# Delta of a masked-softmax graph layer turned by VectorE in 32x32 blocks and dealt through HBM, with the scores placed after the second projection

## The chip, the cores and the metric

The kernel runs on one core of a Trainium2 chip. The metric is the device time of one execution in microseconds. The engines are named as in the profile: PE (TensorE), ACT (ScalarE), DVE (VectorE), POOL (GpSimd) and SP (SyncE, which only issues the DMAs here). The name of an engine with a small q is its sequencer or queue.

## What is computed

32 batches of 256 nodes with 384 features. For each batch, from x (256 x 384) and an adjacency matrix (256 x 256, about 3% ones):

```python
u = h @ h.T / sqrt(384)
p = softmax(u, axis=-1)
delta = p * adjacency
attn = delta / (delta.sum(axis=2, keepdims=True) + 1e-10)
h_left, h_self, h_right = h @ W_left.T + b_left, h @ W_self.T + b_self, h @ W_right.T + b_right
ctx = triu(attn, 1) @ h_left + diag(attn)[:, None] * h_self + tril(attn, -1) @ h_right
o = layernorm(ctx) * gamma + beta          # eps 1e-12
out = layernorm(x + relu(o))               # eps 1e-5
```

Everything is float32. The kernel leaves out the division by the softmax sum and by the row sum of delta: the layer norm that follows is blind to the scale of a row, so only its epsilon is scaled. What PE multiplies is split into a high and a low part (fp32r), and each product is three passes: high by high, high by low, low by high.

## The kernel before

A batch is two row tiles (T = 2) of 128 nodes; features are three chunks (C = 3) of 128. The batches run one after the other in a loop unrolled four times (`every_batch`, UNROLL = 4). Each engine has its own program in a fixed order, in which `at` is the batch at hand, `nxt` the one after it, `before` and `second` the one and the two before; semaphores tie the programs together, and nothing is reordered at run time. So the order of the calls in the five functions `one` is the order of the work.

PE, for each batch (`one`, L329): the left and right projection of row tile 0 (`project` 0 and 1, 9 matmuls of 384 columns each), `turn_delta` (L297: delta is [row, neighbour] and is wanted as [neighbour, row], so four 128x128 blocks are transposed into the PSUM tile ps_dt), projections 2 to 5 (left and right of row tile 1, then self of both), `scores` of the next batch (18 matmuls of 256 columns), and `attend` for both row tiles (9 matmuls of 386 columns each, which accumulate on ps_ctx). A projection starts on a PSUM bank (`ps_proj`, four banks in a ring) that ACT has seeded with the bias (`seed_proj`, L359), and `attend` on a ps_ctx that ACT has seeded with the self projection times the diagonal of delta (`seed_ctx`, L380).

ACT (`one`, L418) writes the high part of each of the first four projections (`split_proj`), of delta transposed (`split_delta`, L376) and of the next batch's x (`split_xt`), seeds the banks, takes the exponentials of the next batch in place (`exps`, L351), normalises the batch before (`normalise`) and writes the output of the second before (`outputs`).

DVE (`one`, L552) writes the low parts, takes the row maxima of the scores (`maxima`), forms delta (`deltas`, L461), sums its diagonal blocks against an identity (`diagonal`), and does the statistics of both layer norms (`context_stats`, `norm_shift`, `residual`, `residual_stats`). POOL (`one`, L634) raises the variances to -1/2 (`power`, tile rstd), multiplies by gamma (scaled), adds beta (shifted), and cuts the two diagonal blocks of delta transposed into strict triangles with two selects (`triangles`, L614; the first matmul of `attend` waits for them).

SP (`one`, L250): once the residual of the second batch before is formed, three loads (x transposed, x, adjacency) into the ring of four; then the store of the second batch's output. Ahead of the loop it issues the first batches' loads and the weights one after the other.

Of the kernel before, what the change touches and what calls it, by code (L numbers as in the profile page):

```python
# [22 lines left out]
P = 128  # L23
UNROLL = 4
# [49 lines left out]
def gnn_resnorm(nc, x, x_t, adj, wt_left, b_left, wt_self, b_self, wt_right, b_right, gamma, beta, out):  # L74
# [14 lines left out]
    BLOCKS = [(0, 0), (1, 1), (1, 0), (0, 1)]  # L89
    FULL, MASK_LEFT, MASK_RIGHT = range(3)  # L90
    ATTEND = [
        [(MASK_LEFT, 0, 0), (MASK_RIGHT, 0, 1), (FULL, 2, 2)],
        [(FULL, 3, 1), (MASK_LEFT, 1, 2), (MASK_RIGHT, 1, 3)],
    ]

    with ExitStack() as ctx:
# [24 lines left out]
        xt_hi = [sb(f"xt_hi{i}", [P, C, L], F32R) for i in range(2)]  # L121
        xt_lo = [sb(f"xt_lo{i}", [P, C, L], F32R) for i in range(2)]
# [8 lines left out]
        on_diag = sb("on_diag", [P, T, P])  # L131

# [14 lines left out]
        rstd = sb("rstd", [P, 2 * T])  # L147
        shift = sb("shift", [P, 2 * T])
# [7 lines left out]
        ps_dt = psum("ps_dt", [P, T * T, P])  # L156
# [22 lines left out]
        dt_ready = sem("dt_ready")  # L179
# [42 lines left out]

        block = ctx.enter_context(nc.Block())

        @block.sync
        def _(sp):
# [16 lines left out]
            for b in range(1, UNROLL):  # L243
                load(b, b)
# [22 lines left out]
        def _(pe):  # L267
# [7 lines left out]
            def xt(at, c, a, b):  # L275
                par = at.slot(2)
# [47 lines left out]
            for _ in range(WARM_UP):  # L324
                nc.tensor.transpose(ps_dt[:, 0, :], ident[:], ident[:])
# [3 lines left out]
            def one(at):  # L329
# [3 lines left out]
                turn_delta(at)  # L333
# [347 lines left out]
```

## Time and profile before

| | us |
|---|---|
| median of 3 runs | 522.84 |
| lowest and highest | 522.25, 522.88 |
| the profiled execution, whole | 522.73 |
| its span in the trace | 521.0 |

| engine | busy us | share of the span | instructions |
|---|---|---|---|
| PE matmul | 498.4 | 96% | 3030 |
| PE weight load | 487.6 | 94% | 3030 |
| DVE | 315.4 | 61% | 844 |
| ACT | 328.6 | 63% | 740 |
| POOL | 236.7 | 45% | 233 |

The first table's 1.73 us between the execution and its span lie outside of what the profile's rows cover. In the second table busy time is an average over the whole span. Matmuls overlap each other in the records (one of 384 columns is shown with 0.34 us, and the next starts 0.17 us after it), so what PE costs is read from starts, or from the chain that ended last, and not from durations. All 16 DMA engines together are busy for 28.5% of the span.

### The profile page before, as it was taken

The page shows a single profiled execution, that of the slowest core. Times are in us where ns is not written, and L with a number is a line of the kernel's source. Part 1 is how long each engine was busy: PE and PEld are TensorE (multiplying, and loading weights), DVE is VectorE, ACT ScalarE, POOL GpSimd, SP SyncE. Part 2 cuts the span into 40 slices and gives each one's busy share as a digit, 9 for nine tenths or more (in the row PEclk, how much of TensorE's full clock was granted, in tenths as well). Part 3 has the DMA queues.
Part 4 walks back from the last instruction along what each step waited for, and adds up shares of the span by engine and source line. Part 5 has one row for each costly group of instructions (what it writes and reads, how often), then busy time and mean ns, then how long its engine had stood idle before and what let it go on. Part 6 is the DMA issues. An engine that isn't in the chain of part 4 may idle for free.

```text
span 521.0 us, 9473 instructions
## 1 busy us (share of the span) xinstructions
PE 498.4 (96%) x3030; PEld 487.6 (94%) x3030; DVE 315.4 (61%) x844; ACT 328.6 (63%) x740; POOL 236.7 (45%) x233
## 2 busy tenths in 40 slices
PE   6899999999999999999999999999999999999980
PEld 6799999999999999999999999999999999999980
DVE  2565666666565656566666556565656666656652
ACT  4655567576667676657667656757565766665642
POOL 0243345553345554344554334555334455433454
PEclk9899999999999999999999999999999999999996
DMA  8802332123333123333112333212333311330001
GB/s 261 274 0 83 112 111 92 52 81 113 111 111 109 36 77 111 111 111 111 66 70 85 111 111 111 103 42 77 111 111 111 111 52 71 100 111 32 31 30 60
DMA packets 40849, 49.11 MB, mean 94 GB/s; under 512 B 2176, under 2 KB 40832, under 8 KB 40832
## 3 DMA queue, kind: packets, MB, share of 16 engines
q1 hardware_dynamic: 40832, 48.90, 28.5%
q8 instruction: 9, 0.15, 0.1%
q14 instruction: 8, 0.07, 0.0%
HBM read 36.31 MB, written 12.58 MB: 94 GB/s over the span
## 4 chain that ended last, share of the span: by engine, by line
POOL 33%; issue 32%; PE 20%; ACT 5%; DVE 5%; DMA 2%; POOLq 1%; SPq 1%; ACTq 0%; DVEq 0%
PE ps_proj L271 12%; POOL scaled L628 11%; POOL shifted L632 9%; POOL dt_right L618 6%; POOL rstd L624 5%; PE ps_ctx L315 5%; ACT normed L391 3%; PE ps_scores L271 2%; POOL dt_left L618 2%; DMA w_raw<-in_L_gnn_W_right 2%; DVE proj_lo L475 1%; DVE shift L511 1%; DVE dt_full L480 1%; PE ps_dt L302 1%; ACT ps_proj L370 1%
## 5 line engine op out<-in xcount | busy, mean ns | idle before, releaser
L271 PE MATMUL ps_proj<-w_hi,xt_hi 128*128 128x384 f32 x576 | 197.0, 342 | 4.3 <-DVE w_lo L532 2.6
L271 PE MATMUL ps_proj<-w_hi,xt_lo 128*128 128x384 f32 x576 | 194.1, 337 | 0.0
L271 PE MATMUL ps_proj<-w_lo,xt_hi 128*128 128x384 f32 x576 | 194.1, 337 | 0.0
L370 ACT ACTIVATE ps_proj<-bias 128x384 f32<-128x384 f32 (+1 forms) x192 | 90.3, 498 | 80.3 <-DVE proj_lo L475 76.4
L624 POOL TENSOR_TENSOR rstd<-var_eps,minus_half 128x4 f32<-128x4 f32 x33 | 33.8, 1024 | 226.2 <-DVE var_eps L504 224.4
L271 PEld LDWEIGHTS ps_proj<-w_hi,xt_hi 128*128 128x128 f32 x576 | 108.6, 189 | 4.8 <-DVE w_lo L532 2.9
L271 PEld LDWEIGHTS ps_proj<-w_lo,xt_hi 128*128 128x128 f32 x576 | 108.6, 189 | 0.0
L271 PEld LDWEIGHTS ps_proj<-w_hi,xt_lo 128*128 128x128 f32 x576 | 108.6, 188 | 0.0
L374 ACT ACTIVATE proj_hi<-ps_proj 128x384 fp32r<-128x384 f32 x128 | 62.8, 491 | 58.5 <-PE ps_proj L271 58.5
L475 DVE TENSOR_TENSOR proj_lo<-ps_proj,proj_hi 128x384 fp32r<-128x384 f32 x128 | 70.7, 553 | 42.0 <-ACT proj_hi L374 38.4
L628 POOL TENSOR_TENSOR scaled<-normed,gamma_sb 128x384 f32<-128x384 f32 x64 | 76.1, 1189 | 34.3 <-ACT normed L391 31.4
L518 DVE SCALAR_TENSOR_TENSOR y_sb<-shifted,x_sb 128x384 f32<-128x384 f32 x64 | 36.5, 570 | 52.5 <-POOL shifted L632 50.5
L632 POOL TENSOR_TENSOR shifted<-scaled,beta_sb 128x384 f32<-128x384 f32 x64 | 65.0, 1015 | 2.6
L391 ACT ACTIVATE normed<-ps_ctx,shift,rstd 128x384 f32<-128x384 f32 x64 | 39.5, 668 | 33.4 <-DVE shift L511 33.4
L271 PE MATMUL ps_scores<-xt_lo,xt_hi 128*128 128x256 f32 x192 | 54.1, 282 | 0.0
L271 PE MATMUL ps_scores<-xt_hi,xt_lo 128*128 128x256 f32 x192 | 54.1, 282 | 0.0
L271 PE MATMUL ps_scores<-xt_hi 128*128 128x256 f32 x192 | 54.1, 282 | 0.0
L485 DVE BATCH_NORM_STATS2 stats<-ps_ctx 128x6 f32<-128x384 f32 x64 | 35.9, 561 | 25.2 <-PE ps_ctx L315 25.2
L315 PE MATMUL ps_ctx<-proj_hi,dt_full 128*128 128x386 f32 x128 | 44.8, 360 | 1.3 <-ACT ps_ctx L385 0.5
L400 ACT ACTIVATE out_sb<-y_sb,shift,rstd 128x384 f32<-128x384 f32 x64 | 41.5, 698 | 5.7 <-DVE shift L511 5.7
L454 DVE TENSOR_TENSOR xt_lo<-xt_sb,xt_hi 128x768 fp32r<-128x768 f32 x32 | 41.2, 1287 | 3.6 <-ACT xt_hi L349 3.6
L315 PE MATMUL ps_ctx<-proj_hi,dt_right 128*128 128x386 f32 x128 | 43.3, 338 | 0.0
(62 smaller groups left out, 732.8 us busy)
## 6 DMA issues: line engine op xcount, KB each, us to landing
xt_sb<-in_x_t SPq DMA_DIRECT2D x32, 384.0 KB, 3.5
x_sb<-in_x SPq DMA_DIRECT2D x32, 384.0 KB, 4.1
out_dram<-out_sb SPq DMA_DIRECT2D x32, 384.0 KB, 2.5
adj_sb<-in_adj SPq DMA_DIRECT2D x32, 256.0 KB, 4.2
w_raw<-in_L_gnn_W_left SPq DMA_DIRECT2D x1, 576.0 KB, 4.2
w_raw<-in_L_gnn_W_right SPq DMA_DIRECT2D x1, 576.0 KB, 8.4
w_raw<-in_L_gnn_W_self SPq DMA_DIRECT2D x1, 576.0 KB, 9.4
bias<-in_L_gnn_b_left SPq DMA_DIRECT2D x1, 192.0 KB, 5.1
```

The costliest lines, as they stand in the source:

```text
L271: mm = nc.tensor.matmul(to, stationary, moving, start=(k == 0 and not seeded), stop=(k == len(passes) - 1), skip_group_check=seeded)
L315: mm = nc.tensor.matmul(ps_ctx[:, t, 0:HE], s, m, start=False, stop=True, skip_group_check=True)
L370: nc.scalar.activation(ps_proj[bank(at, g)][:, 0:to], bias[w][:, 0:to], ACT.Copy).then_inc(proj_seeded, 1)
L374: nc.scalar.activation(proj_hi[:, g, 0:H], ps_proj[bank(at, g)][:, 0:H], ACT.Copy).then_inc(proj_hi_ready, 1)
L391: nc.scalar.activation(normed[:, t, :], ps_ctx[:, t, 0:H], ACT.Identity, bias=shift[:, t:t + 1], scale=rstd[:, t:t + 1]).then_inc(normed_r ...
L400: nc.scalar.activation(out_sb[at.slot(2)][:, t, :], y_sb[at.slot(2)][:, t, :], ACT.Identity, bias=shift[:, T + t:T + t + 1], scale=rstd[:, ...
L454: nc.vector.tensor_tensor(xt_lo[at.slot(2)][:], xt_sb[at.slot(UNROLL)][:], xt_hi[at.slot(2)][:].bitcast(F32), ALU.subtract).then_inc(xt_lo ...
L475: nc.vector.tensor_tensor(proj_lo[:, g, 0:H], ps_proj[bank(at, g)][:, 0:H], proj_hi[:, g, 0:H].bitcast(F32), ALU.subtract).then_inc(proj_l ...
L618: nc.gpsimd.affine_select(out=to[:].rearrange("p h t l -> p h (t l)"), in_=blocks, compare_op=ALU.is_gt, fill=0.0, base=0, pattern=[[0, 2] ...
L624: nc.gpsimd.tensor_tensor(rstd[:], var_eps[:], minus_half[:], ALU.pow).then_inc(rstd_ready, 1)
L628: nc.gpsimd.tensor_tensor(scaled[:, t, :], normed[:, t, :], gamma_sb[:], ALU.mult).then_inc(scaled_ready[t], 1)
L632: nc.gpsimd.tensor_tensor(shifted[:, t, :], scaled[:, t, :], beta_sb[:], ALU.add).then_inc(shifted_ready[t], 1)
```

## The change

- The four transposes on PE and their PSUM tile go. DVE transposes delta instead, right after forming it, with one instruction over [128, 512] that turns each 32x32 block in place of its grid of 4x4 (`turn`, tile turned). A block transposed in this way holds the right numbers in the wrong 32 partitions.
- SP then stores `turned` to a scratch tensor in HBM (dt_dram, 256 KB), waits until it has landed, and loads it back with four DMAs, one for each group of 32 partitions (tile dt_raw, 64 KB each). ACT and DVE make the high and the low part from dt_raw, in SBUF.
- On PE the scores of the next batch move up, to right behind project 1. With them `maxima`, `exps`, `deltas`, `turn` and `diagonal` of the next batch move up on ACT and DVE; `split_xt` is done two batches ahead (xt_hi and xt_lo get four slots in place of two), and several seeds and outputs change places.
- SP's `one` now holds the turn of the next batch between the loads and the store. At the start x transposed of batch 1 is loaded ahead of two of the weights, and batches 2 and 3 are loaded only after the first turn.
- The order of the blocks in delta transposed is now (0,0), (0,1), (1,0), (1,1), so the diagonal blocks are no longer side by side: POOL makes four selects of 256 elements in place of two of 512. rstd and shift get two slots.

```diff
@@ -86,11 +86,14 @@
-    BLOCKS = [(0, 0), (1, 1), (1, 0), (0, 1)]
+    R = 32
+    Q = P // R
-        [(MASK_LEFT, 0, 0), (MASK_RIGHT, 0, 1), (FULL, 2, 2)],
-        [(FULL, 3, 1), (MASK_LEFT, 1, 2), (MASK_RIGHT, 1, 3)],
+        [(MASK_LEFT, 0, 0), (MASK_RIGHT, 0, 1), (FULL, 1, 2)],
+        [(FULL, 2, 1), (MASK_LEFT, 1, 2), (MASK_RIGHT, 1, 3)],
...
-        xt_hi = [sb(f"xt_hi{i}", [P, C, L], F32R) for i in range(2)]
-        xt_lo = [sb(f"xt_lo{i}", [P, C, L], F32R) for i in range(2)]
+        xt_hi = [sb(f"xt_hi{i}", [P, C, L], F32R) for i in range(UNROLL)]
+        xt_lo = [sb(f"xt_lo{i}", [P, C, L], F32R) for i in range(UNROLL)]
...
+        turned = sb("turned", [P, Q * T * T * R])
+        dt_raw = sb("dt_raw", [P, Q, T * T, R])
...
-        rstd = sb("rstd", [P, 2 * T])
-        shift = sb("shift", [P, 2 * T])
+        rstd = [sb(f"rstd{i}", [P, 2 * T]) for i in range(2)]
+        shift = [sb(f"shift{i}", [P, 2 * T]) for i in range(2)]
...
-        ps_dt = psum("ps_dt", [P, T * T, P])
+        ps_warm = psum("ps_warm", [P, P])
...
+
+        dt_dram = nc.dram_tensor("dt_dram", [P, Q * T * T * R], F32, kind="Internal")
+        dt_rows = dt_dram.rearrange("(a c) (q e) -> q c a e", c=R, q=Q)
...
+            def turn(at):
+                sp.wait_ge(turned_ready, at.n(1, 1))
+                sp.dma_start(dt_dram[:], turned[:]).then_inc(turned_stored, 16)
+
+                sp.wait_ge(turned_stored, at.n(16, 16))
+                for q in range(Q):
+                    sp.dma_start(dt_raw[q * R:(q + 1) * R].rearrange("p a k r -> p a (k r)"), dt_rows[q]).then_inc(dt_loaded, 16)
...
@@ -237,10 +258,14 @@
                     for v in range(3):
                         sp.dma_start(bias[v][:, 0:H], biases[v].partition_broadcast(P)).then_inc(biases_loaded, 16)
                     sp.dma_start(adj_sb[0][:], adj_rows[0]).then_inc(adj_loaded[0], 16)
+                    sp.dma_start(xt_sb[1][:], xt_rows[1]).then_inc(xt_loaded[1], 16)
             for to, vector in ((gamma_sb, gamma), (beta_sb, beta)):
                 sp.dma_start(to[:], vector.partition_broadcast(P)).then_inc(vectors_loaded, 16)
-            sp.dma_start(x_sb[0][:], x_rows[0]).then_inc(x_loaded[0], 16)
-            for b in range(1, UNROLL):
+            sp.dma_start(adj_sb[1][:], adj_rows[1]).then_inc(adj_loaded[1], 16)
+            for b in range(2):
+                sp.dma_start(x_sb[b][:], x_rows[b]).then_inc(x_loaded[b], 16)
+            turn(Batch(0, 0))
+            for b in range(2, UNROLL):
                 load(b, b)
...
             def one(at):
-                ahead, behind = at.plus(2), at.plus(-2)
+                ahead, behind, nxt = at.plus(2), at.plus(-2), at.plus(1)
                 if behind.exists(BATCHES):
                     if ahead.exists(BATCHES):
                         sp.wait_ge(y_ready, behind.n(T, T))
                         load(ahead.n(1), ahead.slot(UNROLL))
+                if nxt.exists(BATCHES):
+                    turn(nxt)
+                if behind.exists(BATCHES):
                     store(behind)
...
-            def turn_delta(at):
-                pe.wait_ge(delta_ready, at.n(1, 1))
-                if at.b != 0:
-                    pe.wait_ge(dt_lo_ready, at.n(1, 0))
-                for i, (m, t) in enumerate(BLOCKS):
-                    mm = nc.tensor.transpose(ps_dt[:, i, :], delta[:, t, m * P:(m + 1) * P], ident[:])
-                mm.then_inc(dt_ready, 1)
-
             def attend(at, t):
                 if t == 0:
-                    pe.wait_ge(triangles_ready, at.n(2, 2))
+                    pe.wait_ge(triangles_ready, at.n(2 * T, 2 * T))
...
                 nxt = at.plus(1)
                 project(at, 0)
                 project(at, 1)
-                turn_delta(at)
-                project(at, 2)
-                project(at, 3)
-                project(at, 4)
-                project(at, 5)
                 if nxt.exists(BATCHES):
                     scores(nxt)
+                for g in range(2, NG):
+                    project(at, g)
                 for t in range(T):
                     attend(at, t)
...
             def split_delta(at):
-                act.wait_ge(dt_ready, at.n(1, 1))
-                nc.scalar.activation(dt_full[:, 0, :, :], ps_dt[:], ACT.Copy).then_inc(dt_hi_ready, 1)
+                act.wait_ge(dt_loaded, at.n(64, 64))
+                nc.scalar.activation(dt_full[:, 0, :, :].rearrange("p k (a r) -> p k a r", a=Q),
+                                     dt_raw[:].rearrange("p a k r -> p k a r"), ACT.Copy).then_inc(dt_hi_ready, 1)
...
             exps(first)
+            split_xt(first.plus(1))
             def one(at):
                 nxt = at.plus(1)
-                before, second = at.plus(-1), at.plus(-2)
+                before, second, ahead = at.plus(-1), at.plus(-2), at.plus(2)
                 split_proj(at, 0)
+                split_delta(at)
                 if before.exists(BATCHES):
                     normalise(before)
                 split_proj(at, 1)
-                split_delta(at)
                 seed_proj(at, 4)
                 seed_proj(at, 5)
+                if nxt.exists(BATCHES):
+                    exps(nxt)
                 split_proj(at, 2)
-                if nxt.exists(BATCHES):
-                    split_xt(nxt)
+                split_proj(at, 3)
+                if nxt.exists(BATCHES):
                     seed_proj(nxt, 0)
-                split_proj(at, 3)
+                seed_ctx(at, 0)
+                if nxt.exists(BATCHES):
+                    seed_proj(nxt, 1)
+                if ahead.exists(BATCHES):
+                    split_xt(ahead)
+                seed_ctx(at, 1)
+                if nxt.exists(BATCHES):
+                    seed_proj(nxt, 2)
                 if second.exists(BATCHES):
                     outputs(second)
-                seed_ctx(at, 0)
-                if nxt.exists(BATCHES):
-                    seed_proj(nxt, 1)
-                    seed_proj(nxt, 2)
-                seed_ctx(at, 1)
                 if nxt.exists(BATCHES):
                     seed_proj(nxt, 3)
-                    exps(nxt)
...
+            def turn(at):
+                dve.wait_ge(delta_ready, at.n(1, 1))
+                if at.b != 0:
+
+                    dve.wait_ge(turned_stored, at.n(16, 0))
+                nc.vector.transpose(turned[:].rearrange("p (q k r) -> p k q r", q=Q, k=T * T),
+                                    delta[:].rearrange("p t (h q c) -> p (t h) q c", q=Q, c=R)).then_inc(turned_ready, 1)
...
             def split_delta(at):
                 dve.wait_ge(dt_hi_ready, at.n(1, 1))
-                nc.vector.tensor_tensor(dt_full[:, 1, :, :], ps_dt[:], dt_full[:, 0, :, :].bitcast(F32),
+                lo, hi = (dt_full[:, half, :, :].rearrange("p k (a r) -> p k a r", a=Q) for half in (1, 0))
+                nc.vector.tensor_tensor(lo, dt_raw[:].rearrange("p a k r -> p k a r"), hi.bitcast(F32),
                                         ALU.subtract).then_inc(dt_lo_ready, 1)
...
             deltas(first)
+            turn(first)
             dve.wait_ge(ident_ready, 1)
+            diagonal(first)
+            split_xt(first.plus(1))
...
             def one(at):
                 before, second = at.plus(-1), at.plus(-2)
-                nxt = at.plus(1)
+                nxt, ahead = at.plus(1), at.plus(2)
                 if before.exists(BATCHES):
                     context_stats(before, 1)
                     norm_variances(before)
                     norm_var_eps(before, before.n(T, T), second.n(T, T) if second.exists(BATCHES) else None)
-                diagonal(at)
+                split_proj(at, 0)
                 if before.exists(BATCHES):
                     norm_shift(before)
-                split_proj(at, 0)
+                split_delta(at)
                 split_proj(at, 1)
-                split_delta(at)
+                if nxt.exists(BATCHES):
+                    maxima(nxt)
                 if before.exists(BATCHES):
                     residual(before, 0)
                     residual_stats(before, 0)
+                if nxt.exists(BATCHES):
+                    deltas(nxt)
+                    turn(nxt)
                 split_proj(at, 2)
-                if nxt.exists(BATCHES):
-                    split_xt(nxt)
+                split_proj(at, 3)
+                if nxt.exists(BATCHES):
+                    diagonal(nxt)
                 if before.exists(BATCHES):
                     residual(before, 1)
                     residual_stats(before, 1)
+                if ahead.exists(BATCHES):
+                    split_xt(ahead)
+                if before.exists(BATCHES):
                     dve.wait_ge(stats2_ready, before.n(T, T))
-                split_proj(at, 3)
+                context_stats(at, 0)
                 if before.exists(BATCHES):
                     residual_moments(before)
-                if nxt.exists(BATCHES):
-                    maxima(nxt)
-                context_stats(at, 0)
-                if nxt.exists(BATCHES):
-                    deltas(nxt)
...
-                blocks = dt_full[:, :, 0:T, :].bitcast(F32).rearrange("p h t l -> p h (t l)")
-                for to, sign in ((dt_left, 1), (dt_right, -1)):
-                    nc.gpsimd.affine_select(out=to[:].rearrange("p h t l -> p h (t l)"), in_=blocks, compare_op=ALU.is_gt, fill=0.0, base=0,
-                                            pattern=[[0, 2], [0, T], [-sign, P]], channel_multiplier=sign
-                                            ).then_inc(triangles_ready, 1)
+                for t in range(T):
+                    for to, sign in ((dt_left, 1), (dt_right, -1)):
+                        nc.gpsimd.affine_select(out=to[:, :, t, :], in_=dt_full[:, :, (T + 1) * t, :].bitcast(F32), compare_op=ALU.is_gt,
+                                                fill=0.0, base=0, pattern=[[0, 2], [-sign, P]], channel_multiplier=sign
+                                                ).then_inc(triangles_ready, 1)
...
```

## Rows read from the trace of the kernel before

**Rows 1.** The page: busy tenths and granted TensorE clock in 40 slices of 13 us, and DMA rate.

```profile
PE   6899999999999999999999999999999999999980
PEclk9899999999999999999999999999999999999996
GB/s 261 274 0 83 112 111 92 52 81 113 111 111 109 36 77 111 111 111 111 66 70 85 111 111 111 103 42 77 111 111 111 111 52 71 100 111 32 31 30 60
```

**Rows 2.** The chain that ended last: start us, us, what; batches 30 and 31.

```profile
477.67 3.14 PE ps_proj L271 x18
480.81 0.44 PE ps_dt L302 x4
481.25 6.24 PE ps_proj L271 x36
487.49 2.14 PE ps_scores L271 x18
489.63 3.42 PE ps_ctx L315 x18
493.05 3.14 PE ps_proj L271 x18
...
502.86 3.18 PE ps_ctx L315 x18
```

**Rows 3.** Who waited for whom, 200 to 264 us: us in total, times, longest.

```profile
ACT ps_proj L370 <- DVE proj_lo L475: 10.1, 8, 2.2
...
DVE y_sb L518 <- POOL shifted L632: 6.0, 4, 1.5
...
PEld ps_ctx L315 <- ACT ps_ctx L385: 1.3, 4, 0.4
```

**Rows 4.** Timeline of ACT and DVE, 200 to 217 us: start us, us [idle before <-releaser].

```profile
203.19 1.23 ACT L391 ACTIVATE normed<-ps_ctx,shift,rstd 128x384 f32<-128x384 f32 x2 [0.94 <-DVE shift L511]
...
205.16 0.93 ACT L370 ACTIVATE ps_proj<-bias 128x386 f32<-128x386 f32 x2
...
213.14 0.54 ACT L385 ACTIVATE ps_ctx<-ps_proj,diag 128x386 f32<-128x386 f32 x1
...
214.13 0.19 ACT L353 ACTIVATE neg_max<-row_max 128x2 f32<-128x2 f32 x1
...
215.41 0.69 DVE L464 TENSOR_TENSOR delta<-ps_scores,adj_sb 128x512 f32<-128x512 f32 x1 [1.12 <-ACT ps_scores L356]
```

**Rows 5.** Groups by line and shape: busy us, mean ns of one, idle before.

```profile
L475 DVE TENSOR_TENSOR proj_lo<-ps_proj,proj_hi 128x384 fp32r<-128x384 f32 x128 | 70.7, 553 | 42.0 <-ACT proj_hi L374 38.4 <-DVE stats L523 1.7
L480 DVE TENSOR_TENSOR dt_full<-ps_dt,dt_full 128x512 fp32r<-128x512 f32 x32 | 22.1, 692 | 0.3 <-ACT dt_full L378 0.3
L618 POOL TENSOR_SCALAR_AFFINE_SELECT dt_right<-dt_full 128x512 fp32r<-128x512 f32 x32 | 41.9, 1311 | 0.0
L618 POOL TENSOR_SCALAR_AFFINE_SELECT dt_left<-dt_full 128x512 fp32r<-128x512 f32 x32 | 20.4, 637 | 2.4 <-DVE dt_full L480 2.4
```

**Rows 6.** Tile out_dram: from a 384 KB store's issue to its landing.

```profile
DMA to landing us min/median/max: 2.4/2.5/2.6
```

**Rows 7.** SP's timeline and the page's DMA issues: KB each, us to landing.

```profile
103.36 0.48 SPq L229 DMA_DIRECT2D x_sb<-in_x  x1
104.03 0.37 SPq L230 DMA_DIRECT2D adj_sb<-in_adj  x1
...
adj_sb<-in_adj SPq DMA_DIRECT2D x32, 256.0 KB, 4.2
```

**Rows 8.** Timeline of ACT, DVE and PE, start to the second batch.

```profile
12.20 1.16 ACT L415 ACTIVATE w_hi<-w_raw 128x1152 fp32r<-128x1152 f32 x1 [0.71 <-DMA w_raw<-in_L_gnn_W_right]
...
14.81 0.44 PE L271 MATMUL ps_proj<-w_hi,xt_hi 128*128 128x384 f32 x1 [2.60 <-DVE w_lo L532]
...
16.78 0.69 DVE L464 TENSOR_TENSOR delta<-ps_scores,adj_sb 128x512 f32<-128x512 f32 x1 [1.43 <-ACT ps_scores L356]
...
17.53 1.12 PE L302 MATMUL ps_dt<-ident,delta 128*128 128x128 f32 x4 [0.55 <-DVE delta L464]
...
21.97 0.96 DVE L454 TENSOR_TENSOR xt_lo<-xt_sb,xt_hi 128x768 fp32r<-128x768 f32 x1 [0.17 <-ACT xt_hi L349]
...
30.52 0.34 PE L271 MATMUL ps_proj<-w_hi,xt_hi 128*128 128x384 f32 x1
```

More of the change, by code:

```diff
@@ L178, in gnn_resnorm @@
         scores_ready = sem("scores_ready")
-        dt_ready = sem("dt_ready")
+        turned_ready = sem("turned_ready")
+        turned_stored = sem("turned_stored")
+        dt_loaded = sem("dt_loaded")
         proj_ready = sem("proj_ready")
@@ L275, in xt @@
             def xt(at, c, a, b):
-                par = at.slot(2)
+                par = at.slot(UNROLL)
                 return xt_hi[par][:, c, a:b], xt_lo[par][:, c, a:b]
@@ L324, in _ @@
             for _ in range(WARM_UP):
-                nc.tensor.transpose(ps_dt[:, 0, :], ident[:], ident[:])
+                nc.tensor.transpose(ps_warm[:], ident[:], ident[:])
             first = Batch(0, 0)
@@ L348, in split_xt @@
                 act.wait_ge(xt_loaded[at.slot(UNROLL)], at.loads(UNROLL, 1))
-                nc.scalar.activation(xt_hi[at.slot(2)][:], xt_sb[at.slot(UNROLL)][:], ACT.Copy).then_inc(xt_hi_ready, 1)
+                nc.scalar.activation(xt_hi[at.slot(UNROLL)][:], xt_sb[at.slot(UNROLL)][:], ACT.Copy).then_inc(xt_hi_ready, 1)
             def exps(at):
@@ L390, in normalise @@
                 for t in range(T):
-                    nc.scalar.activation(normed[:, t, :], ps_ctx[:, t, 0:H], ACT.Identity, bias=shift[:, t:t + 1],
-                                         scale=rstd[:, t:t + 1]).then_inc(normed_ready, 1)
+                    nc.scalar.activation(normed[:, t, :], ps_ctx[:, t, 0:H], ACT.Identity, bias=shift[at.slot(2)][:, t:t + 1],
+                                         scale=rstd[at.slot(2)][:, t:t + 1]).then_inc(normed_ready, 1)
             def outputs(at):
+                nxt = at.plus(1).slot(2)
                 act.wait_ge(shift_ready, at.n(1, 2))
@@ L400, in outputs @@
                     nc.scalar.activation(out_sb[at.slot(2)][:, t, :], y_sb[at.slot(2)][:, t, :], ACT.Identity,
-                                         bias=shift[:, T + t:T + t + 1], scale=rstd[:, T + t:T + t + 1]
+                                         bias=shift[nxt][:, T + t:T + t + 1], scale=rstd[nxt][:, T + t:T + t + 1]
                                          ).then_inc(out_ready, 1)
@@ L424, in one @@
                 split_proj(at, 1)
-                split_delta(at)
                 seed_proj(at, 4)
                 seed_proj(at, 5)
+                if nxt.exists(BATCHES):
+                    exps(nxt)
                 split_proj(at, 2)
+                split_proj(at, 3)
                 if nxt.exists(BATCHES):
-                    split_xt(nxt)
                     seed_proj(nxt, 0)
-                split_proj(at, 3)
-                if second.exists(BATCHES):
-                    outputs(second)
                 seed_ctx(at, 0)
@@ L437, in one @@
                     seed_proj(nxt, 1)
-                    seed_proj(nxt, 2)
+                if ahead.exists(BATCHES):
+                    split_xt(ahead)
                 seed_ctx(at, 1)
                 if nxt.exists(BATCHES):
+                    seed_proj(nxt, 2)
+                if second.exists(BATCHES):
+                    outputs(second)
+                if nxt.exists(BATCHES):
                     seed_proj(nxt, 3)
-                    exps(nxt)
             every_batch(act, BATCHES, one)
@@ L453, in split_xt @@
                 dve.wait_ge(xt_hi_ready, at.n(1, 1))
-                nc.vector.tensor_tensor(xt_lo[at.slot(2)][:], xt_sb[at.slot(UNROLL)][:],
-                                        xt_hi[at.slot(2)][:].bitcast(F32), ALU.subtract).then_inc(xt_lo_ready, 1)
+                nc.vector.tensor_tensor(xt_lo[at.slot(UNROLL)][:], xt_sb[at.slot(UNROLL)][:],
+                                        xt_hi[at.slot(UNROLL)][:].bitcast(F32), ALU.subtract).then_inc(xt_lo_ready, 1)
             def maxima(at):
@@ L510, in norm_shift @@
                 dve.wait_ge(rstd_ready, at.n(1, 1))
-                nc.vector.scalar_tensor_tensor(shift[:], moments[:, :, 0], -1.0, rstd[:], ALU.mult, ALU.mult
+                nc.vector.scalar_tensor_tensor(shift[at.slot(2)][:], moments[:, :, 0], -1.0, rstd[at.slot(2)][:], ALU.mult, ALU.mult
                                                ).then_inc(shift_ready, 1)
@@ L614, in triangles @@
             def triangles(at):
[L616 to L620 removed]
+                for t in range(T):
[3 more added lines that the diff above has]
+                                                ).then_inc(triangles_ready, 1)
             def power(at):
                 pool.wait_ge(var_eps_ready, at.n(1, 1))
[L624 removed]
+                nc.gpsimd.tensor_tensor(rstd[at.slot(2)][:], var_eps[:], minus_half[:], ALU.pow).then_inc(rstd_ready, 1)
             def gamma_of(at, t):
```

1 line of the change is left out of this document (removed).

## Prediction

> **What bounds the kernel now.** I read the slices of the page first. From 26 us to the last slice but one PE is busy in nine tenths or more and its clock is at full (2.4 GHz); only the start and the end are thinner, and the clock dips in the second slice [rows 1]. So PE is the engine to follow, and what counts is when its next piece starts. The chain that ended last gives its pieces for one batch: 3.14 us for projections 0 and 1, 0.44 for the four transposes, 6.24 for the other four, 2.14 for the scores, 3.42 for the two attends: 15.38 us from 477.67 to 493.05 [rows 2]. Over thirty batches, from the first projection of batch 1 at 30.52 [rows 8] to that of batch 31 at 493.05 [rows 2], the mean period is 462.53 / 30 = 15.42.
>
> Not all of it is matmul. The last batch's attends take 3.18, the others' 3.42 [rows 2]. The waits say why: PE's load for ps_ctx waits for ACT's ps_ctx, 1.3 us over four batches [rows 3]. The timeline follows it back: ACT seeds ps_ctx for the second row tile at 213.14 to 213.68, more than an attend behind PE's need [rows 4]. ACT is late since the two bank seeds in front wait for DVE's proj_lo (10.1 us in eight waits), and DVE for POOL's shifted (6.0 in four) [rows 3]. That is about 0.3 us of each batch that PE does not work.
>
> **Removed.** The transposes cost PE 0.44 us a batch [rows 2]. The wait for the seed: in the new order DVE writes proj_lo 3 ahead of the second residual, so the seed waits for PE's projection alone, and ACT has only one bank seed and xt_hi in front of it. If all of it goes, a batch costs 3.14 + 6.24 + 2.14 + 3.18 = 14.70, 0.72 less than the mean. Thirty batches give 21.6, the last one its 0.44: **22.0 us off**. The selects, the doubled rstd and the two more xt slots touch no PE time.
>
> **Is there room for what is added?** I put batch `at` at 0 to 14.7 and walk. Scores of the next batch end at 3.14 + 2.14 = 5.3. Maxima (0.7, like any DVE row over 512 elements [rows 5]) end near 6.1. neg_max to the end of delta took 214.13 to 216.10 = 1.97 [rows 4]: 8.1. The 32x32 transposition is in no row. It streams 512 elements; its nearest rows are the DVE operations of that size, 0.69 [rows 5]. Its bounds are half and twice of that, 0.35 and 1.4, since it has one source but writes in runs of 32. With 0.69 it ends near 8.9.
>
> The Trainium skill ("VectorE: DVE Perf Modes", The three transpose paths and Rules for kernel authors) advises TensorE for a 128x128 transposition whose destination may be PSUM, which speaks against this change, and gives 0.31 us for 128x128 bf16 on VectorE; four such would be 1.24, an estimate from that page, inside my bounds. No run shows it yet.
>
> The round trip: a store of 384 KB lands 2.4 to 2.6 us after its issue [rows 6]; this one has 256 KB, and I take 2.4. SP issues DMAs 0.67 apart, with 0.37 to 0.48 for one issue [rows 7]: three gaps are 1.1 to 2.0, I take 1.5. Loads land after at most 4.2 at the median, with 768 KB in front of them in the queue [rows 7]; a small one behind nothing is nearer to the store row, 2.4. Together **6.3 us, between 2.3** (issues alone, 0.4 and 5 x 0.37) **and 8.8** (2.6 + 2.0 + 4.2). The data is back at 8.9 + 6.3 = 15.2, that is 0.5 into the next batch. ACT asks for it at 1.7 + 0.4 = 2.1, behind the high part of projection 0. So at the likely value ACT does not wait.
>
> The new waits block two engines. SP waits for `turned` and for its landing; queued behind are the store and then the next three loads. These are asked for only a batch later, and in the walk SP reaches them when the output is ready (near 14), as before. On ACT the wait for dt_loaded stands in front of normalise, proj_hi 1, seeds 4 and 5, and the exponentials. From normed to the end of the two seeds ACT took 203.19 to 206.09 = 2.9, with split_delta in it [rows 4]. PE needs seed 4 at 3.14 + 2.14 + 3.12 = 8.4, so the data may come as late as 5. The tighter limit is the loop through the next turn: 2.9 + 0.4 (proj_lo 1 before seed 5) + 1.97 + 0.69 + 0.2 for some five semaphores = 6.2, plus the round trip, must fit in 14.7. **The round trip decides from 8.5 us on**; every 0.1 above costs 31 x 0.1.
>
> POOL: four selects of 256 elements for two of 512; at 0.64 for 512 [rows 5] and a fixed part of at most half, they are 1.3 to 2.6 together. The last ends near 9 to 10, and the attend needs it at 11.5. The low part of delta now reads SBUF twice. The select beside DVE's xt_lo, which does so too, takes 1.31 where the same work takes 0.64 [rows 5]; so this may cost POOL up to 0.7, inside that slack. DVE gains 0.7 of work a batch and is at 61%; ACT gains none.
>
> **The start pays.** x transposed of batch 1 (384 KB) goes ahead of the weights of the right and the self projection; at 261 to 274 GB/s [rows 1] that is 1.5 us. So everything from ACT's w_hi at 12.20 moves by 1.5: the second projection from 14.81 to 16.3, delta from 16.78 to 18.3 [rows 8]. Turned at 19.6; diagonal 0.5; xt_lo of batch 1 at 1.0 [rows 8] ends at 21.1, and only then do the scores of batch 1 begin: PE, done with projection 1 near 18, stands for 3 us. The round trip is bare here: 19.6 + 6.3 = 25.9. Then ACT: high part of delta, proj_hi 1, seeds 4 and 5 with the wait for proj_lo, 2.2 to 28.1; exponentials and delta of batch 1, 1.97 and 0.2 for semaphores, 30.3; transposition 31.0; proj_lo 2 (0.55 [rows 5]) 31.6; bank seed and ctx seed 32.6; both attends 3.18: **35.8 in place of 30.52**, 5.3 late. The clock: it is low in the second slice [rows 1], where PE had been idle 2.60 [rows 8]; the new gaps are longer, and pieces of 3.1 and 2.1 us could run at 1.2 GHz, 0 to 4 more. Much of it hides behind the round trip; I take 0.5. Start: **+5.8, from 3 to 10**.
>
> The end is the same chain of norms: no change.
>
> **Sum.** Span 521.0 - 22.0 + 5.8 = 504.8; with the 1.7 outside the span (522.73 - 521.0) 506.5. The profiled execution lies 0.1 under the median of the runs, which I neglect.
>
> **The rivals.**
> *The seed wait stays.* DVE's low parts, or ACT's xt_hi in front of the ctx seed, are again late for the second attend. For: both engines work in order, and the slack is short: projection 5 is readable at 3.14 + 2.14 + 6.24 + 0.2 = 11.7, ACT's xt_hi in front ends near 11.9, the ctx seed (0.54 [rows 4]) at 12.4, and PE needs it one attend after 11.5, at 13.1. Against: 0.7 is more than the 0.3 that was missing before. Then only 0.44 a batch is gained: 521.0 + 1.7 - 14.1 + 5.8 = 514.4. Chance 0.13.
>
> *The round trip takes the place of the transposes, and the kernel is slower.* Place: ACT's wait for dt_loaded. It decides from 8.5 us, and the gain of 16.2 is gone when 31 x the excess reaches it, near 9.0 (the start then loses more too). With both landings at 4.2 and 2.0 of issues it is 10.4: 31 x 1.9 = 59, 4 more at the start, 570. Against: the DMA engines are idle at that point, as the input loads were issued half a batch earlier. Its hard form: the four loads pass one after the other, 2.6 + 4 x 2.4 = 12.2, 3.7 too long, 31 x 3.7 = 115 and 6 at the start, 627. Against: in the steady state three loads issued within 1.1 us land within 4.2 each. Chance 0.09, of which 0.03 for the hard form.
>
> The Trainium skill ("DMA: Bandwidth & Descriptors", Rules for kernel authors) says that two transfers to disjoint partition halves serialize, and asks for one 128-partition transfer; taken for whole DMAs it would be that hard form, and taken for bandwidth alone it changes nothing here. The same page fits one DMA as 2.0 us plus the bytes at 436 GB/s (SWDGE): 2.6 for the store and 2.15 for a load, by which the round trip is 6.3, an estimate from that page.
>
> *It does what it says but PE was not the only thing in the period*: some other wait of 0.1 to 0.2 a batch appears, 510 to 513; in the forecast's range.
>
> **How the numbers follow.** Forecast (no PE wait in the loop, start +3 to +10, up to 0.2 a batch): 0.74, 502 to 513, likeliest 506.5. Seed wait stays 0.13. Slower 0.09. Start cheaper and better than 502: 0.04. The range 500 to 516 takes in all but the slower rival and its neighbourhood. The measurement can tell about 0.2% from no change, 1 us: faster 0.88, same 0.02, slower 0.10.
>
> **What would show it.** Right: ps_dt gone from the chain; period of projection 0 at 14.7; no wait of PE for ps_ctx; ACT's dt_full without idle time in the loop but with some 6 us in the first batch; projection 0 of batch 1 near 36; dt_raw's last landing 6.3 us after turned. Wrong: ACT dt_full waiting for DMA dt_raw in every batch (round trip over 8.5), a transposition of over 1.4, or PE idle before ps_ctx or a projection.

## The result, and the profile after

The changed kernel takes 505.15 us (median of 5 runs, 504.49 to 508.25), the kernel before 522.71 on the same chip: a ratio of 0.968 (95% interval 0.965 to 0.971). The forecast was 506.5, from 500 to 516. The profiled execution took 508.25, with a span of 506.5.

The page after: the busy tenths and the granted clock of PE in 40 slices of 12.7 us.

```profile
PE   7579999999999999999999999999999999999980
PEclk9889999999999999999999999999999999999995
```

Against [rows 1], the thin part at the start is longer: the second and third slices hold five and seven tenths, and the clock is down in both. The rest is full.

The chain that ended last, in order of time (start us, us, what): the first batches, one batch of the middle, and the start of the last.

```profile
28.14 3.37 PE ps_proj L299 x18
31.51 1.88 issue
33.39 4.97 PE ps_ctx L335 x18
38.36 3.18 PE ps_proj L299 x18
...
199.98 3.12 PE ps_proj L299 x18
203.10 2.14 PE ps_scores L299 x18
205.25 6.25 PE ps_proj L299 x36
211.50 3.17 PE ps_ctx L335 x18
...
479.02 9.36 PE ps_proj L299 x54
```

A batch is 3.12 + 2.14 + 6.25 + 3.17 = 14.68 us. ps_dt is gone, and the attends take 3.17 where they took 3.42 [rows 2]. From the first projection of batch 1 at 38.36 to that of batch 31 at 479.02 the mean period is 440.66 / 30 = 14.69. So against the span of before: 521.0 - 21.87 (thirty periods) - 0.44 (the last batch) + 7.84 (batch 1 begins at 38.36, not 30.52 [rows 8]) = 506.5. The tail is unchanged.

The timeline of the loop (start us, us, engine, line; projection 0 of this batch began at 199.98):

```profile
201.97 0.62 ACT L395 ACTIVATE dt_full<-dt_raw 128x512 fp32r<-128x512 f32 x1
...
205.57 1.01 POOL L666 TENSOR_TENSOR scaled<-normed,gamma_sb 128x384 f32<-128x384 f32 x1
205.89 1.11 DVE L550 SCALAR_TENSOR_TENSOR y_sb<-shifted,x_sb 128x384 f32<-128x384 f32 x1
...
207.94 0.40 POOL L656 TENSOR_SCALAR_AFFINE_SELECT dt_right<-dt_full 128x256 fp32r<-128x256 f32 x1
208.32 0.71 DVE L494 STREAM_TRANSPOSE turned<-delta 128x512 f32<-128x512 f32 x1
...
209.06 0.35 SPq L247 DMA_DIRECT2D dt_dram<-turned  x1
...
211.10 1.76 SPq L251 DMA_DIRECT2D dt_raw<-dt_dram  x4
...
211.69 0.54 ACT L403 ACTIVATE ps_ctx<-ps_proj,diag 128x386 f32<-128x386 f32 x1
```

`turned` ends at 9.05 in the batch. The store lands 2.04 after that, four loads go out 0.44 apart, and the last lands 2.0 after its issue (page rows below): 2.04 + 1.3 + 2.0 = 5.4 us, so the data is there near 214.4. ACT asks for it 14.7 after 201.97, at 216.65: 2.2 us to spare. Of 200 to 259 us no wait of PE is listed.

The page's DMA issues (KB each, median us to landing), and the groups by line and shape (busy us, mean ns | idle before):

```profile
dt_dram<-turned SPq DMA_DIRECT2D x32, 256.0 KB, 2.0
dt_raw<-dt_dram SPq DMA_DIRECT2D x128, 64.0 KB, 2.0
```

```profile
L494 DVE STREAM_TRANSPOSE turned<-delta 128x512 f32<-128x512 f32 x32 | 22.8, 712 | 3.3
L550 DVE SCALAR_TENSOR_TENSOR y_sb<-shifted,x_sb 128x384 f32<-128x384 f32 x64 | 53.7, 839 | 4.7 <-POOL shifted L670 4.7
L512 DVE TENSOR_TENSOR dt_full<-dt_raw,dt_full 128x512 fp32r<-128x512 f32 x32 | 21.9, 686 | 5.4 <-ACT dt_full L395 5.4
L395 ACT ACTIVATE dt_full<-dt_raw 128x512 fp32r<-128x512 f32 x32 | 20.0, 625 | 7.0 <-DMA dt_raw<-dt_dram 7.0
```

The last row decides the main rival: 7.0 us of waiting for dt_raw in 32 batches. The timeline of the start says where that is:

```profile
14.07 1.16 ACT L434 ACTIVATE w_hi<-w_raw 128x1152 fp32r<-128x1152 f32 x1 [2.16 <-DMA w_raw<-in_L_gnn_W_right]
...
18.66 0.69 DVE L487 TENSOR_TENSOR delta<-ps_scores,adj_sb 128x512 f32<-128x512 f32 x1 [1.43 <-ACT ps_scores L373]
...
26.60 0.63 ACT L395 ACTIVATE dt_full<-dt_raw 128x512 fp32r<-128x512 f32 x1 [6.97 <-DMA dt_raw<-dt_dram]
```

All of it is in batch 0, whose round trip nothing covers.

### The profile page after: what moved, and what is told of

The parts are those of the page before. It is cut to its first block, busy times and chain, and to the rows that moved or that the text cites. A ratio compares the mean times of both kernels' runs of the same rounds, so it can differ in the third digit from the quotient of the medians.

```text
span 506.5 us, 9515 instructions
## 1 busy us (share of the span) xinstructions
PE 479.6 (95%) x2902; PEld 477.7 (94%) x2902; DVE 339.9 (67%) x876; ACT 334.3 (66%) x740; POOL 220.6 (44%) x297
## 4 chain that ended last, share of the span: by engine, by line
PE 91%; DMA 3%; DVE 1%; ACT 1%; POOL 1%; SPq 1%; issue 1%; POOLq 0%; ACTq 0%; DVEq 0%
PE ps_proj L299 58%; PE ps_ctx L335 20%; PE ps_scores L299 13%; DMA w_raw<-in_L_gnn_W_right 2%; DMA dt_raw<-dt_dram 1%; POOL shifted L670 0%; DMA dt_dram<-turned 0%; POOL scaled L666 0%; DVE w_lo L564 0%; SPq L259 0%; SPq L251 0%; ACT w_hi L434 0%; POOLq L99 0%; ACT ps_scores L373 0%; POOL rstd L662 0%
## 5 line engine op out<-in xcount | busy, mean ns | idle before, releaser
L299 PE MATMUL ps_proj<-w_hi,xt_hi 128*128 128x384 f32 x576 | 194.4, 337 | 6.9 <-DVE w_lo L564 4.1
L387 ACT ACTIVATE ps_proj<-bias 128x384 f32<-128x384 f32 (+1 forms) x192 | 94.1, 492 | 29.8 <-DVE proj_lo L506 26.4
L506 DVE TENSOR_TENSOR proj_lo<-ps_proj,proj_hi 128x384 fp32r<-128x384 f32 x128 | 67.2, 544 | 59.1 <-ACT proj_hi L391 59.1
L666 POOL TENSOR_TENSOR scaled<-normed,gamma_sb 128x384 f32<-128x384 f32 x64 | 64.7, 1011 | 36.4 <-ACT normed L409 36.4
L550 DVE SCALAR_TENSOR_TENSOR y_sb<-shifted,x_sb 128x384 f32<-128x384 f32 x64 | 53.7, 839 | 4.7 <-POOL shifted L670 4.7
L335 PE MATMUL ps_ctx<-proj_hi,dt_left 128*128 128x386 f32 x128 | 43.5, 340 | 1.9 <-issue 1.9
L477 DVE TENSOR_TENSOR xt_lo<-xt_sb,xt_hi 128x768 fp32r<-128x768 f32 x32 | 30.7, 959 | 16.4 <-ACT xt_hi L366 16.4
```

The costliest lines, as they stand in the source:

```text
L299: mm = nc.tensor.matmul(to, stationary, moving, start=(k == 0 and not seeded), stop=(k == len(passes) - 1), skip_group_check=seeded)
L335: mm = nc.tensor.matmul(ps_ctx[:, t, 0:HE], s, m, start=False, stop=True, skip_group_check=True)
L387: nc.scalar.activation(ps_proj[bank(at, g)][:, 0:to], bias[w][:, 0:to], ACT.Copy).then_inc(proj_seeded, 1)
L506: nc.vector.tensor_tensor(proj_lo[:, g, 0:H], ps_proj[bank(at, g)][:, 0:H], proj_hi[:, g, 0:H].bitcast(F32), ALU.subtract).then_inc(proj_l ...
L550: nc.vector.scalar_tensor_tensor(y_sb[at.slot(2)][:, t, :], shifted[:, t, :], 0.0, x_sb[at.slot(UNROLL)][:, t, :], ALU.max, ALU.add).then_ ...
L666: nc.gpsimd.tensor_tensor(scaled[:, t, :], normed[:, t, :], gamma_sb[:], ALU.mult).then_inc(scaled_ready[t], 1)
```

## The experiments

Theory: the gain is 0.44 us a batch of transposes and 0.28 of the late seed, both by themselves; the round trip and DVE's work lie under slack of a size that can be measured; and the start pays some 6 us. Rivals: the new order does it all or nothing of it; the round trip or DVE is already at its edge. Ratios are to the kernel before, measured beside each run, with 95% intervals. In the code cuts `...` stands for lines left out, and the comments are added here. All ten kernels compute the whole result; some add work that nothing reads.

**The order alone.** PE's transposes come back behind project 1, everything else stays as changed.

```diff
+                turn_delta(at)        # PE: four transposes to ps_dt
...
-            turn(first)               # DVE, and SP's store and loads
```

> The changed kernel with PE's four transposes put back behind projection 1, and no transposition on DVE, no store and no loads for it; the new order of all engines is kept. It splits the 0.73 us a batch that the change gained (15.42 to 14.69). Theory (0.44 are the transposes, 0.28 the wait for the ctx seed that the new order removed): period 14.69 + 0.44 = 15.13, 31 batches 13.6 us more, and a start without the round trip. In the trace of the changed kernel ACT stands 6.97 us for it in the first batch; without it the seeds and the attend come at least 3 us earlier. Total 505.2 + 13.6 - 3 to 5 = 514 to 516. Rival (the ctx seed's wait comes back as soon as PE holds the transposes, so the whole gain belongs to the DMA): period 15.4, total about 519 to 522.

515.72 us (0.987, 0.985 to 0.989). Its chain in the middle:

```profile
200.25 3.13 PE ps_proj L289 x18
203.38 0.44 PE ps_dt L320 x4
...
212.21 3.17 PE ps_ctx L333 x18
```

The period is 15.13: 0.29 under 15.42, with attends of 3.17. So the order cures the late seed by itself, and the transposes are worth 0.44 a batch in the loop (15.13 to 14.69). The changed kernel gives part of that back at its start: here batch 1 begins at 33.85, there at 38.36.

**The DMA turn in the old order.** The kernel before with the new turn, and the four selects that go with it, in place of PE's transposes.

> The kernel before with the turn on DVE and through HBM, but all engines in the old order (scores at the end of a batch); SP turns a batch ahead of its loads. Theory (the early scores are what hides the round trip): delta of a batch is there only about 0.7 us into that batch, turned 0.7 later, and the data is back 5.4 after that (2.04 store, three issues 0.44 apart, 2.0 for a load in the trace of the changed kernel), at 6.8; ACT then still has the high part, 0.6, and the seeds 4 and 5 to write, to 8, while PE wants the first at 6.3. PE waits 1.6 to 2.2 us a batch, beside the ctx seed wait of 0.3: period 16.3 to 17.0, total 550 to 575. Rival (the gain is the removed transposes, wherever the scores stand): period 15.0, total about 510 to 515.

611.48 us (1.171, 1.168 to 1.174), worse than expected. The period is 17.78 at this place (17.96 in the mean of thirty), and the chain is no longer PE's:

```profile
206.10 2.02 DMA dt_dram<-turned
...
211.47 0.64 ACT dt_full L386
...
212.99 1.19 POOL scaled L648
216.33 0.99 POOL shifted L652
...
223.89 2.02 DMA dt_dram<-turned
```

The round trip is the 5.4 of the changed kernel, but 12.4 us of other work stand in the same circle: the selects come between POOL's scaled and shifted, and the residual, a proj_lo, ACT's two seeds and the exponentials stand in front of the next delta. In the old order the turn does not pay; the two parts of the change cannot be priced one by one and added. The new order moves more than the scores, and no run moved the scores alone.

**A longer round trip.** SP stores a tile to scratch space once, or twice, and waits for it, between the landing of `turned` and the loads.

```diff
                 sp.wait_ge(turned_stored, at.n(16, 16))
+                sp.dma_start(pad_dram[:], adj_sb[at.slot(UNROLL)][:].rearrange('p t l -> p (t l)')).then_inc(pad_stored, 16)
+                sp.wait_ge(pad_stored, at.n(16, 16))
```

> The changed kernel with one more store of 256 KB to a spare tensor in HBM, whose landing SP awaits between the landing of the turned delta and the four loads: the round trip grows by the 2.0 us of such a store, from 5.4 to 7.4. Theory (the round trip decides from 8.5 us on): the period stays 14.69, only the start pays 2.0: total 507 to 508. Rival (the round trip is on the path of every batch, and each microsecond counts): 31 x 2.0 more, 567.

> As the run before with two such stores one after the other: the round trip grows to 9.4 us. Theory (limit 8.5): 0.9 us a batch too long, period 15.6, 28 us in the loop and 4 at the start: total 537, slower than the kernel before. Rival (the loop has more room than I think, the limit is above 9.4): period 14.69, total 509 to 510.

One more: 509.57 us (0.976, 0.975 to 0.978), 3 to 4 more than the changed kernel, with a period of 14.69 in the middle as before. The loop still has room at 7.4 us, but little: ACT waits for dt_raw in nine batches (in one without the pad), and one round trip, from 91.52 to 100.15, took 8.6, since its first store landed only after 2.8. In this profile batch 1 begins at 36.67, no later than in the changed kernel, as the weights came early; the loss is in the batches right behind it. Batches 1 and 2 take 15.82 and 15.16, and batches 5 and 6, around the slow round trip, 14.90 and 15.12. Batch 1 waits:

```profile
48.20 0.86 issue
49.06 3.43 PE ps_ctx L339 x18
```

Two more: 564.04 us (1.080, 1.078 to 1.082) where 537 was expected. Its chain:

```profile
201.12 2.03 DMA dt_dram<-turned
...
203.17 2.03 DMA pad_dram<-adj_sb
...
208.53 2.12 DMA dt_raw<-dt_dram
...
211.21 0.67 ACT normed L415
...
211.95 1.02 POOL scaled L672
...
213.05 1.02 POOL shifted L676
...
214.09 1.36 DVE y_sb L556
...
215.95 0.69 DVE delta L493
...
217.49 2.02 DMA dt_dram<-turned
```

A period of 16.37 (16.39 in the mean of thirty), of which 9.53 is round trip (201.12 to 210.65, dt_full's start). The other 6.84 is not the way I had drawn. I had sent the circle through ACT's seeds and exponentials; it goes through normalise to POOL's scaled and shifted and to DVE's residual, which stands in front of delta. The limit is therefore 14.70 - 6.84 = 7.9 us, not 8.5. That is a difference of measured times; no run had a round trip between 7.4 and 9.5 in every batch.

**The start.** First, x transposed of batch 1 is loaded behind the weights again. Second, batch 0 alone is turned by PE, the others by DMA. Third, both. Beside them the changed kernel once more.

```diff
-                    sp.dma_start(xt_sb[1][:], xt_rows[1]).then_inc(xt_loaded[1], 16)
+            sp.dma_start(xt_sb[1][:], xt_rows[1]).then_inc(xt_loaded[1], 16)   # behind the loop over weights
```

```diff
-            turn(Batch(0, 0))
...
+                if at.b == 0:
+                    turn_first()      # PE: four transposes to ps_dt, read by split_delta of batch 0
```

> The changed kernel with x transposed of batch 1 loaded behind the weights of the right and the self projection, as it was before the change, in place of ahead of them. In the two traces the weight of the right projection reaches ACT at 12.20 before and at 14.07 after. Theory (this delay of 1.9 us runs through the start: second projection, maxima, delta, turn): the start is 1.9 us shorter, total 503.2. Rival (x transposed of batch 1 then comes too late for the early scores, and the start gains nothing): 505 to 507.

> The changed kernel with batch 0 alone turned by PE's four transposes (behind projection 1), all other batches through HBM. Theory (the bare round trip of batch 0 is the larger part of what the start pays): ACT, which stands 6.97 us for dt_raw in the first batch, writes the high part at about 20 in place of 26.6; PE runs from the scores at 20.8 through four projections (6.25) and scores (2.15) to the attends at 29.2, and projection 0 of batch 1 begins near 32.4 in place of 38.4 in the profiled execution, which was itself 3 us above the median. Against the median 3 to 4 us: total 501 to 502. Rival (the start is set by weights and xt_lo, and PE's clock): under 1 us, 504.5.

> Both changes of the start together: x transposed of batch 1 behind the weights, and batch 0 turned by PE. Theory: the two gains add, 1.9 + 3.5, total near 499.8, since the one moves the start of the chain and the other takes a wait out of it. Rival (both act on the same wait): no better than the better of the two, 501 to 503.

> The changed kernel as it is, on the same chip as the three runs before it, as the yardstick for differences of 2 to 5 us. Expected 505.2; the profiled execution may lie up to 3 us above that, as the first one did (508.25 to 504.49 over five), which I lay to PE's clock in the start: its two pieces of matmuls between the gaps run at one or the other level.

| kernel | median us | ratio to before | batch 1 begins at |
|---|---|---|---|
| changed, again | 506.66 | 0.969 (0.966 to 0.971) | 36.74 |
| weights first | 504.34 | 0.965 (0.964 to 0.966) | 36.02 |
| batch 0 on PE | 502.48 | 0.962 (0.960 to 0.963) | 33.83 |
| both | 501.27 | 0.959 (0.958 to 0.960) | 32.95 |

Against the changed kernel beside them the gains are 2.3, 4.2 and 5.4, where 1.9, 3 to 4 and 5.4 were expected. How nearly they add is not shown: this yardstick scattered from 504.43 to 507.92, and the same kernel had a median of 505.15 the first time, against which the gains are 0.8, 2.7 and 3.9. The first gain is not clear of that noise (the intervals of the first two rows touch, and its profiled execution shows 0.7); the other two are. The totals lie 0.5 to 1.5 us above the expected ones. The last kernel is the fastest of all here. The chains around the attends of batch 0, first of the changed kernel again, then of the one with both:

```profile
29.98 1.89 issue
31.87 4.87 PE ps_ctx L335 x18
36.74 3.21 PE ps_proj L299 x18
```

```profile
19.48 3.41 PE ps_scores L300 x18
22.89 6.87 PE ps_proj L300 x36
29.76 3.19 PE ps_ctx L342 x18
32.95 3.18 PE ps_proj L300 x18
```

In the second there is no gap in front of the attends and they run at full speed. The slow stretch is not gone, though: it has moved to the scores and projections in front of them, 3.41 and 6.87 where the loop has 2.14 and 6.25, so 1.9 us more, about what the attends lose in the first (4.87 for 3.18). What the kernel with both gains is idle time of PE, and weights that come 1.0 us earlier (12.63, against 13.64). From the start of batch 1 to the end the spans leave the same time in all: 504.9 - 36.74 = 468.2, 501.1 - 32.95 = 468.2, and 506.5 - 38.36 = 468.1 in the first profile of the changed kernel. So the start explains both these gains and the 1.6 us between the two profiled executions of the changed kernel. I had laid that scatter to PE's clock, and the profiles show otherwise: the attends lose the same in both (4.97 and 4.87). The weights came at 14.07 and 13.64, 0.4 apart, and the last load of dt_raw landed 3.1 us after its issue in the first and 2.0 in the second, 1.1 apart.

**More work on DVE.** delta is transposed into spare tiles once, or three times, ahead of the real one.

```diff
+                nc.vector.transpose(spare0[:].rearrange("p (q k r) -> p k q r", q=Q, k=T * T),
+                                    delta[:].rearrange("p t (h q c) -> p (t h) q c", q=Q, c=R))
```

> The changed kernel with a second, unused transposition of delta (to a spare tile) ahead of the one that is stored: 0.63 us more on DVE in every batch, from the start of one transposition to the next instruction in the trace of the changed kernel. Theory (DVE has room of 0.88 us there: proj_lo 2 and 3 stand behind the transposition, the bank seed and the ctx seed on ACT behind them, and the ctx seed ended at 210.62 where PE wanted it at 211.50): period stays 14.69, the start pays once, total 0.7 above the changed kernel, 506. Rival (DVE's added work is on the path): 31 x 0.63 = 20 more, 525.

> As the run before with three unused transpositions: 1.9 us more on DVE in every batch. The round trip's limit would allow it: that loop closes at a round trip of 7.9 us, as the run with two more stores showed (6.8 us of work beside the DMAs), and 5.4 + 1.9 = 7.3. Theory (proj_lo 2 and the ctx seed bind first, with 0.88 of room): 1.0 us a batch too late, period 15.7, total 505.5 + 31 + 2 = 538, with PE idle before ps_ctx for ACT's seed. Rival (only the round trip's loop counts): period 14.69, total 508.

Twice: 507.25 us (0.970, 0.968 to 0.971), periods of 14.68 to 14.76, 14.72 in the mean: hidden, all but 0.03 us. Four times: 543.88 (1.041, 1.038 to 1.043), where 538 was expected, a period of 15.88 for 15.7. Of its timeline:

```profile
208.10 0.49 ACT L388 ACTIVATE ps_proj<-bias 128x384 f32<-128x384 f32 x1 [2.35 <-DVE proj_lo L513]
208.53 0.54 ACT L404 ACTIVATE ps_ctx<-ps_proj,diag 128x386 f32<-128x386 f32 x1
...
209.19 0.44 PE L336 MATMUL ps_ctx<-proj_hi,dt_left 128*128 128x386 f32 x1 [0.85 <-ACT ps_ctx L404]
```

This is the rival of the seed wait, provoked: DVE's proj_lo comes late behind the transpositions, ACT's bank seed waits 2.35 for it, the seed of ps_ctx stands behind that, and PE waits. Three more cost DVE 0.59 each from start to start, 1.8 in all, and the period grows by 1.19: DVE had about 0.6 us to spare, not 0.88. The run with one more, 0.6, sits at that edge.

## Why the prediction was right, point by point

- *PE bounds, and the transposes and the seed wait go.* Right, and each shown alone: the transposes 0.44, the seed wait 0.29 by the order. Thirty periods and the last batch's transposes gave 22.3 for 22.0. One reading on the way was off: ACT's second ps_ctx seed, which ended at 213.68, was not more than an attend behind PE's need but 0.15 behind it, since the attends had begun at 211.94 and one takes 1.59.
- *The transposition, 0.69 between 0.35 and 1.4.* 0.712, so its nearest row, the DVE operation of the same size, was a good price; the other estimate, 1.24, was too high. The Trainium skill ("VectorE: DVE Perf Modes", Rules for kernel authors) advises TensorE where the result may go to PSUM; this kernel disagrees, by 515.72 with PE's transposes against 505.15 and 506.66 with DVE's, in the same order. PE was the bound and DVE was not.
- *The walk.* `turned` ends at 9.05 (8.9 forecast), the ctx seed at 12.25 (12.4), the last select at 8.4 (9 to 10). The four selects took 1.9 together; with a fixed part of at most half, the sum for them should have been 1.3 to 1.9, not 2.6.
- *The round trip, 6.3.* 5.4 in the loop: both landings 2.0, not 2.4, and the issues 0.44 apart, 1.3 in place of 1.5. In batch 0 it was 6.5 in the first profile and 5.4 in the second. The likeliest term was 0.9 high, on the safe side, and so was the second way to 6.3, with 2.6 for the store and 2.15 for a load.
- *The limit, 8.5.* Mis-sized: 7.9. I had drawn one circle through the wait for dt_loaded, over ACT; POOL's scaled and shifted and the residual in front of delta make a longer one. At 5.4 it does not matter; at 8.2 I would have forecast the whole gain, where 8.2 + 6.84 = 15.04 leaves about half of it. So the total came out right although this step did not.
- *The hard form, four loads one after the other.* Did not occur. The last load is issued 1.3 us behind the first and lands 2.0 later, 3.3 in all; one after the other they would be 8. The Trainium skill ("DMA: Bandwidth & Descriptors", Rules for kernel authors) says that transfers to disjoint partition halves serialize; for loads of 64 KB these rows show their latencies overlapping, so here the sentence can hold for bandwidth alone.
- *POOL may lose 0.7 beside the low part of delta.* It did not: POOL has no work there (its rstd ends at 202.39, its scaled begins at 203.51, and the low part runs from 202.65 to 203.34), and dt_full's low part takes 686 ns (692 before, from PSUM [rows 5]). The contention went elsewhere: y_sb, which also reads SBUF twice, takes 839 ns in the mean where it took 570, the one beside POOL's scaled took 1.11 (205.89 above), and the select that began beside it took 0.72 for 0.40. That belongs to the new order and not to the turn: with PE's transposes in the same order y_sb takes 949. xt_lo went the other way, 959 for 1287.
- *The start, +5.8.* It was 7.8 in the profiled execution and 6.2 in the second profile. The weights cost 1.87 (14.07 against 12.20) for 1.5, but these are two single executions: in the eight profiles with the loads in the new order ACT begins on them at 12.93 to 14.32, in the four with the old order at 11.73 to 12.87, 1.2 apart in the mean. Delta came at 18.66 for 18.3, data back at 26.6 for 25.9, the attends at 33.4 for 32.6. The mis-sized term is the clock: I gave it 0.5, and the attends of batch 0 alone took 4.97 in place of 3.18, 1.8 more; the other 0.8 had gathered before them. Here are the windows of the trace after (us, then busy us and count of PE, PEld, DVE, ACT, POOL, then granted clock, DMA share, GB/s):

```profile
34.00:37.00 3.00, 3.00 (x11) 3.00 (x11) 1.52 (x2) 1.73 (x4) 0.00 (x0) 0.51 0.25 73
60.00:120.00 60.00, 60.00 (x369) 60.00 (x368) 43.17 (x111) 41.94 (x95) 28.29 (x40) 1.00 0.42 132
```

PE is busy without a break from 34 to 37 and yet at a granted clock of 0.51 (1.00 from 60 to 120), the lower of its two levels (1.2 GHz). Ahead of the attends lay idle stretches of 1.18 us (up to 28.14) and 1.88 (up to 33.39), with PE at full clock between them. The fall came after the work had begun again: the first four matmuls of the attends start 0.18 to 0.25 apart, those from 34.28 to 37.18 about 0.32 apart, and the last ones from 37.48 on 0.18 again. I had argued that such a loss would hide behind the round trip. It did for projection 1 of batch 0, which ran from 16.68 with 0.32 from start to start, while the scores behind it ran at full clock; but the attends come after the round trip.

In the profiled execution the loop gained 0.3 more and the start lost 2.0 more than forecast: 506.5 - 0.3 + 2.0 = 508.2, measured 508.25. In the second profile the start lost 0.4 more: 506.6, measured 506.66. The median of the first five runs, 505.15, lies under both; what the start took in the runs without a profile is not known. That the median lies only 1.4 from the forecast is in part luck: the start alone moved by 1.6 between two profiles of one kernel.

## What to carry to other kernels

When one engine is busy without a break, moving even 0.44 us a batch off it pays in full in every batch of the loop, if the longer way around lies under slack; find the circle that contains the detour, add up all of it over every engine that works in order, and compare it with the period. Take the reordering and the detour as one change: here the order alone gave 1.3%, both 3.2%, and the detour alone cost 17%. A detour that is hidden in the loop is bare in the first batch, so let that batch keep the old way: here that gave 0.8%, and 1.1% with the loads in their old order, against the changed kernel measured beside them.

## What the runs showed of the hardware

- A store of 256 KB from SBUF to HBM and a load of 64 KB back both landed 2.0 us after issue at the median, and four loads issued 0.44 apart did not queue behind each other. The longest took 3.7; the last load of batch 0, with loads of 384 KB issued right behind it, took 3.1.
- One VectorE transposition of 32x32 blocks over 128x512 fp32 took 0.71 us, and 0.59 from start to start when several follow each other, through a rearranged output.
- The clock of PE can fall while PE is busy: idle for 1.2 and 1.9 us at the start, PE then worked for 0.7 us at full clock and some 3.2 at half (granted 0.51 from 34 to 37), and came back to full without a break in its work. With both changes of the start, which close the gap in front of the attends, a slow stretch lay in the scores and projections instead.
- Of a DVE operation with two inputs in SBUF and a POOL operation beside it, the one that began second took longer. y_sb takes 0.56 us alone; begun 0.3 us behind POOL's scaled it took 1.11 (205.89), begun 0.1 behind it 1.36 (214.09 with two more stores). In the kernel before, y_sb began first, at 206.07, and took its 0.56, and scaled, begun at 206.09, took 1.41 for 1.01. The traces show the order and the times, not the reason; no run took POOL's operation away alone.
